# Last attention weights of the second batch: exponentials with a bias by head, then turned, and a new order of work on all engines

## The reference, cut to what matters

```python
q = (x @ Wq).reshape(b, t, h, dh)      # 8 heads of 64
k = (x @ Wk).reshape(b, t, h, dh)
gl_v = (x @ Ws).reshape(b, t, h, e)
wv = _topk_mask(gl_v, 2) * sigmoid(gl_v)
v = einsum('bthe,btek->bhtk', wv, einsum('btd,edk->btek', x, Wv))
scores = einsum('bhid,bhjd->bhij', q * scale, k)
probs = softmax(scores, axis=-1)
attn = einsum('bhij,bhjd->bihd', probs, v)
mask_o = _topk_mask((x @ Wd).reshape(b, t, h, e), 2)
out = einsum('bthe,bthk,ekd->btd', mask_o, attn, Wo)
```

## Time and profile before

| | us |
|---|---|
| median of three runs | 231.01 (230.71 to 776.88) |
| the profiled execution's own time | 230.83 |
| its span in the profile | 229.1 |
| PE busy in the span | 220.0 |
| DVE, ACT, POOL busy | 166.0, 101.1, 93.4 |

### The profile page before, as it was taken

The page is one execution under the profiler, slowest core; times in us unless marked ns, Lnnn a source line. Parts: engine busy times, 40 slices in busy tenths (PEclk is TensorE's granted clock), DMA queues, the critical chain, the costliest instruction groups (busy, mean ns, idle before and its releaser), DMA issues.

```text
span 229.1 us, 3195 instructions
## 1 busy us (share of the span) xinstructions
PE 220.0 (96%) x1192; PEld 167.7 (73%) x1192; DVE 166.0 (72%) x311; ACT 101.1 (44%) x196; POOL 93.4 (41%) x89
## 2 busy tenths in 40 slices
PE   8999999999999899999989999999999699999995
PEld 8998898889888688879474444444557488998963
DVE  2156387767579899981773484899988899698971
ACT  2256425375489497614145245597512202160310
POOL 5104203655566821971025616744863127330000
PEclk9999999999999999999999999999999999999999
DMA  6999859966968973099983298000000000000011
GB/s 235 429 412 399 358 185 451 393 263 215 379 235 318 413 322 137 0 342 419 429 313 150 78 339 363 0 0 0 1 0 3 0 0 3 0 0 4 0 43 49
DMA packets 6639, 43.99 MB, mean 192 GB/s; under 512 B 864, under 2 KB 1376, under 8 KB 1760
## 3 DMA queue, kind: packets, MB, share of 16 engines
q1 hardware_dynamic: 6480, 43.66, 48.2%
q10 hardware_dynamic: 144, 0.13, 0.2%
HBM read 43.27 MB, written 0.52 MB: 191 GB/s over the span
## 4 chain that ended last, share of the span: by engine, by line
PE 69%; DVE 26%; issue 2%; ACT 1%; DVEq 0%; POOL 0%; POOLq 0%
PE psum L412 49%; PE psum L454 16%; DVE ring_r L939 5%; PE psum L428 2%; DVE slots_r L1049 1%; PE psum L416 1%; DVE small L1042 1%; DVE slots L921 1%; DVE slots L1140 1%; ACT slots L1596 1%; PE psum L580 1%; DVE small L911 1%; DVE slots_r L1037 1%; DVE slots L927 1%; DVE psum L1063 1%
## 5 line engine op out<-in xcount | busy, mean ns | idle before, releaser
L412 PE MATMUL psum<-ring_r,slots_r 128*128 128x512 f32 x288 | 69.8, 396 | 2.0 <-DVE slots_r L1109 1.5
L412 PEld LDWEIGHTS psum<-ring_r,slots_r 128*128 128x128 f32 x288 | 53.0, 188 | 15.2 <-ACT slots_r L1596 2.1
L412 PE MATMUL psum<-ring,slots 128*128 128x512 f32 (+5 forms) x170 | 61.4, 513 | 0.7 <-DVE slots L1266 0.5
L1921 POOL TENSOR_TENSOR ring_r<-ring,ring_r 128x640 fp32r<-128x640 f32 x18 | 36.3, 2028 | 43.2 <-ACT ring_r L1596 43.1
L1596 ACT ACTIVATE slots<-psum 128x256 f32<-128x256 f32 (+4 forms) x48 | 20.7, 455 | 71.3 <-PE psum L412 32.4
L412 PEld LDWEIGHTS psum<-ring,slots 128*128 128x128 f32 (+1 forms) x170 | 29.3, 190 | 28.3 <-issue 25.5
L1596 ACT ACTIVATE ring_r<-ring 128x2048 fp32r<-128x2048 f32 x20 | 37.9, 1912 | 7.7 <-PE psum L412 6.8
L454 PE MATMUL psum<-slots,ring 128*128 128x128 f32 x320 | 37.5, 276 | 0.5 <-ACT slots L1596 0.5
L454 PEld LDWEIGHTS psum<-slots,ring 128*128 128x128 f32 x320 | 36.5, 192 | 1.2 <-ACT slots L1596 0.9
L939 DVE TENSOR_TENSOR ring_r<-ring,ring_r 128x1408 fp32r<-128x1408 f32 x18 | 30.2, 1692 | 2.5 <-ACT ring_r L1596 2.3
L1916 POOL TENSOR_TENSOR small<-small,mhalf 128x1 f32<-128x1 f32 x16 | 10.6, 663 | 36.0 <-DVE small L913 34.5
(11 more groups left out here) (184 smaller groups left out, 244.2 us busy)
## 6 DMA issues: line engine op xcount, KB each, us to landing
ring<-blocks SPq DMA_DIRECT2D x36, 1024.0 KB, 8.6
bc<-vecs SPq DMA_DIRECT2D x1, 3072.0 KB, 15.1
bc<-vecs SPq DMA_DIRECT2D x1, 1280.0 KB, 6.6
bc<-vecs SPq DMA_DIRECT2D x1, 512.0 KB, 13.7
slots<-xin SPq DMA_DIRECT2D x1, 256.0 KB, 5.2
y<-slots SPq DMA_DIRECT2D x1, 256.0 KB, 2.0
y<-slots SPq DMA_DIRECT2D x2, 128.0 KB, 1.8
slots<-xin ACTq DMA_DIRECT2D x1, 128.0 KB, 2.7
```

Source lines behind the costliest of these rows:

```text
L412: return t.matmul(o_, l, r, start=first, stop=last)
L1921: g.tensor_tensor(ring_r[:, p, CUT:], ring[:, p, CUT:], ring_r[:, high(name), CUT:], ALU.subtract).then_inc(*split_lowg.inc(name))
```

## The change

Three things are done together.

First, batch 1's last weights are made as batch 0's: `score_t`, `turn_max`, `less_max`, `max_parts`, `select`, `max_turned` and `exp_p` go, with their constants; `max_f`, the exponentials with a bias (`exp_f_`), the turning (`turn_weights`) and the copy out (`weights_out`) serve both batches.

```diff
+            def turn_weights(b, q):
+                s.wait_ge(*exp_f[b].at(str(q)))
                 s.wait_ge(*gates_a[b].at("xv"))
                 s.wait_ge(*gates_a[b].at("k"))
                 s.wait_ge(*gates_v[b].at("gl"))
+                transposes(bank(4 * b + 2 * q), P0[b][:, q * 512:(q + 1) * 512]).then_inc(*sf[b].inc(f"turn{q}"))
...
             def max_f(b, q):
                 s.wait_ge(*sf[b].at(str(q)))
+                v.tensor_reduce(mxf[b][:, 4 * q:4 * q + 4], quarters(4 * b + (1 if q else 3)), AX.X,
+                                ALU.max).then_inc(*own_v.inc())
+                s.wait_ge(*own_v.now())
+                v.tensor_scalar(nmx[b][:, 4 * q:4 * q + 4], mxf[b][:, 4 * q:4 * q + 4], -0.125, None,
+                                ALU.mult).then_inc(*smax_v[b].inc(str(q)))
...
+            def exp_f_(b, q):
+
+                s.wait_ge(*smax_v[b].at(str(q)))
                 for c in range(4):
                     n = 4 * q + c
+                    i = act(P0[b][:, n * 128:(n + 1) * 128],
+                            psum[:, 4 * b + (1 if q else 3), c * 128:(c + 1) * 128], ACT.Exp,
+                            bias=nmx[b][:, n:n + 1], scale=0.125)
+                i.then_inc(*exp_f[b].inc(str(q)))
+
+            def weights_out(b, q):
+                s.wait_ge(*sf[b].at(f"turn{q}"))
+                act(PTf[b][:, q * 512:(q + 1) * 512], bank(4 * b + 2 * q), ACT.Copy).then_inc(*w_out[b].inc(str(q)))
```

Second, the orders of the last block (TensorE, VectorE, ScalarE):

```diff
+            score_f(0, 1)
             score_f(0, 0)
-            score_f(0, 1)
             fk(1)
-            turn_p0(1)
-            turn_p0(0)
+            turn_weights(0, 0)
+            turn_weights(0, 1)
             score_f(1, 0)
+            av(0, 0)
             score_f(1, 1)
             av(0, 1)
-            av(0, 0)
-            turn_max(1)
-            score_t(1)
-            less_max(1)
-            sum_u(0, 1)
+            turn_weights(1, 0)
+            turn_weights(1, 1)
             av(1, 0)
             sum_u(0, 0)
             av(1, 1)
+            sum_u(0, 1)
+            fo(0, 0)
             sum_u(0, 2)
-            fo(0, 0)
             fo(0, 1)
             fo(0, 2)
             sum_u(1, 0)
             sum_u(1, 1)
+            fo(1, 0)
             sum_u(1, 2)
-            fo(1, 0)
...
             p0_turned()
             max_f(1, 0)
+            out_gate(0, 0)
+            gate_out(0, 2, 0)
             max_f(1, 1)
-            max_parts(1)
+            gate_out(0, 0, 0)
             out_gate(0, 1)
-            out_gate(0, 0)
+            gate_out(0, 0, 1)
             gate_out(0, 1, 0)
             gate_out(0, 1, 1)
-            gate_out(0, 0, 0)
-            gate_out(0, 0, 1)
-            gate_out(0, 2, 0)
             gate_out(0, 2, 1)
             out_gate(1, 0)
+            out_gate(1, 1)
+            gate_out(1, 1, 0)
             gate_out(1, 0, 0)
-            gate_out(1, 1, 0)
-            out_gate(1, 1)
             gate_out(1, 0, 1)
             gate_out(1, 1, 1)
+            final(0)
             gate_out(1, 2, 0)
             gate_out(1, 2, 1)
-            final(0)
             final(1)
...
             fq_out(0)
-            exp_p0(0)
-            exp_p0(1)
+            fk_out(0)
             fq_out(1)
+            exp_f_(0, 1)
+            exp_f_(0, 0)
             fk_out(1)
-            select()
-            p0_turned()
-            max_turned(1)
-            exp_p(1, 0)
-            exp_p(1, 1)
+            weights_out(0, 0)
+            exp_f_(1, 0)
+            exp_f_(1, 1)
+            weights_out(1, 0)
+            weights_out(1, 1)
```

Third, the work ahead of the last block is put in another order on all five lists, its amount unchanged: SP's fetches, TensorE's biases, steps and scores, and much of the lists of the others. SP's part from `ct13` on, and TensorE's around `f1(1)`:

```diff
             fetch("ct13")
             fetch("c02")
             fetch("c00")
+            fetch("c01")
             fetch("c11")
+            fetch("c10")
             fetch("c03")
-            fetch("c13")
-            fetch("c10")
             fetch("c12")
             fetch("f1")
+            fetch("f2")
+            fetch("c13")
+            fetch("rg")
+            fetch("ra")
+            fetch("fq")
             fetch("rk")
+            fetch("rv")
+            fetch("ro")
+            s.wait_ge(*used("c12"))
+            fetch("fg")
             s.wait_ge(*used("c11"))
             fetch("rf")
             fetch("rr")
...
             f2(0)
-            s.wait_ge(*normed[1].at("x2"))
-            in_halves(1, "x2", Z[1], 7, 5)
-            f1(1)
-            s.wait_ge(*p_low[1].at("3"))
-            s.wait_ge(*evict[1].at("relu"))
-            bias("a0", 6)
             s.wait_ge(*p_low[0].at("3"))
             s.wait_ge(s_bc1, 16)
             s.wait_ge(*turned[0].at("x2"))
             bias("a0", 1)
+            s.wait_ge(*normed[1].at("x2"))
+            in_halves(1, "x2", Z[1], 7, 5)
+            f1(1)
             turned_rows(0, "n4", N4[0], 0)
             f2(1)
+            step(0, "k", 1, 2)
             step(0, "a", 0, 1, bias_of="a0")
-            step(0, "k", 1, 2)
+            turned_rows(1, "n4", N4[1], 4)
+            s.wait_ge(*p_low[1].at("3"))
+            s.wait_ge(*evict[1].at("relu"))
+            bias("a0", 6)
             s.wait_ge(*normed[1].at("x3"))
             bias("w0", 7)
-            turned_rows(1, "n4", N4[1], 4)
-            step(0, "v", 2, 3, wait=normed[0].at("x3"))
-            step(1, "k", 0, 5, wait=evict[1].at("relu"))
             s.wait_ge(*mixed[0].at("a"))
             s.wait_ge(*mixed[0].at("k"))
             step(0, "r", 3, 0, wait=turned[0].at("n4"))
+            step(1, "k", 0, 5, wait=evict[1].at("relu"))
+            step(0, "v", 2, 3, wait=normed[0].at("x3"))
             step(1, "a", 1, 6, bias_of="a0")
```

More of the change, by code:

```diff
@@ L191, in build @@
         vt2 = [slot(R[b][5]) for b in range(2)]
-        P0 = slot(R[0][0], 2)
+        P0 = [slot(R[b][0], 2) for b in range(2)]
         PTf = [slot(R[b][2], 2) for b in range(2)]
@@ L750, in _ @@
             k1(0)
+            turned_rows(1, "x", Y[1], 4)
             q1(0)
-            turned_rows(1, "x", Y[1], 4)
+            k1(1)
             e1(0)
@@ L789, in _ @@
             scores(1, 3)
-            gather(0, 0)
-            count2(1)
             turn_p(0, 2)
             turn_p(0, 3)
+            count2(1)
+            gather(0, 0)
             shut_out(1)
@@ L1795, in _ @@
             copy_halves(0, "x1", T8, 0, 2)
+            split("ct00")
             out(1, "v1", Vs[1], bank(5))
@@ L1946, in _ @@
                             pattern=[[-1, 128]], channel_multiplier=1).then_inc(*const.inc("ident"))
+            g.memset(mhalf[:, :], -0.5).then_inc(*const.inc("mhalf"))
+            deviation(0, "x")
+            deviation(1, "x")
+            g.memset(causal[:, :], 0.0).then_inc(*own_g.inc())
+            s.wait_ge(*own_g.now())
+            g.affine_select(out=causal[:, :], in_=causal[:, :], compare_op=ALU.is_ge, fill=NEG, base=0,
+                            pattern=[[-1, 128]], channel_multiplier=1).then_inc(*const.inc("causal"))
+            g.memset(pick, 0.0).then_inc(*own_g.inc())
+            g.iota(kidx[:, :], pattern=[[1, 128]], base=0, channel_multiplier=0,
+                   allow_small_or_imprecise_dtypes=True).then_inc(*const.inc("kidx"))
+            low("v1")
+            low("ct01")
+            deviation(0, "x1")
+            low("ct00")
+            g.iota(kidx4[:, :], pattern=[[1, 512]], base=0, channel_multiplier=512,
+                   allow_small_or_imprecise_dtypes=True).then_inc(*const.inc("kidx4"))
+            low("ct02")
             s.wait_ge(*own_g.now())
@@ L1995, in _ @@
             deviation(1, "x2")
-            deviation(0, "x3")
-            deviation(0, "n4")
-            low_third("ro", 0)
             s.wait_ge(*normed[1].at("x2"))
@@ L2001, in _ @@
             mul(x2b[1], Z[1], vec("fc2_b"), x2b_g[1], "x2b", ALU.add)
+            deviation(0, "x3")
+            deviation(0, "n4")
+            low_third("ro", 1)
             deviation(1, "x3")
             deviation(1, "n4")
-            for base in (0, -8):
-                s.wait_ge(*own_g.now())
-                i = g.affine_select(out=sel, in_=sel, compare_op=ALU.not_equal, fill=-1.0, base=base,
-                                    pattern=[[-1, 8]], channel_multiplier=1)
-                i.then_inc(*(const.inc("sel") if base else own_g.inc()))
-            low_third("ro", 1)
+            s.wait_ge(*normed[0].at("n4"))
+            s.wait_ge(s_bc2, 16)
+            mul(X[0], X[0], vec("lnf_b"), x_off[0], "s", ALU.add)
+            g.memset(wbias[:, :], WC).then_inc(*const.inc("wbias"))
             low_third("ro", 2)
+            s.wait_ge(*rk_v[0].at("ys"))
+            mul(sc_[0], ys[0], vec("r_k"), rk_g[0], "sb")
             s.wait_ge(*evict[1].at("k"))
```

429 lines of the change are left out of this document (165 added, 264 removed), and 4 rows, old and new, of the table prod.

## The result

The changed kernel took **234.44 us** (median; 233.78 to 234.93), the kernel before 230.86 in the runs beside it. The ratio is 1.0138 with an interval of 1.0108 to 1.0168: slower by 1.4%, where 230.2 us was forecast, 0.8 less than the 231.01 that the prediction started from. Of the four runs of the kernel before beside it, one of 776.88 stands apart. The profiled execution took 234.68 us.

The account below looks back on a forecast made before the run. TensorE was taken as the bound nearly everywhere. Last block -0.6 and middle -0.2 sum to -0.8: span 229.1 to 228.3, plus 1.73 around it 230.0, plus 0.18 gives 230.2 us (own range 229.4 to 231.2; with rivals 228.4 to 232.6).

Parts of the forecast that it names:

- Last block: Batch 1's new weights path at the end: less TensorE work (-1.73), one wait gone (-0.46), new waits added; -0.6 taken.
- the timetable: Last block's steps on TensorE, VectorE and ScalarE from 204.66, giving waits of 0.35 and 1.05 before batch 1's turns.
- rival 3: VectorE and ScalarE set the end, by scalings of 1.18 or waits per quarter: +1.4 there, 232.2 us; chance 0.17.
- Early: New order in the early part: later `x1` turning against a covered wait before `shut_out(1)`; 0 together, from -0.6 to +0.5.
- The half microsecond for `x1`: Early part: `k1(1)` ahead of `e1(0)` delays `pv1(0)`, so TensorE reaches `x1`'s turning before VectorE has it: +0.5.
- `low_third("rf", 0)` behind `deviation(0, "h")`: GpSimd's order near `h`: the low third still ends before `rf(0)` needs it, by about 0.8 us.
- Middle: One bias fewer ahead of the steps at 131.40: -0.35, of which 0.2 is kept after batch 1's `yg`; bounds -0.5 and +0.5.
- Fetches: Weight blocks behind `fq`, at 423 GB/s: `rr` lands at 129.4, wanted at 131.05; cost 0, 1.7 us of cover.
- the sign named for being wrong about rival 2: TensorE or ScalarE showing a wait for a DMA between 115 and 145 in the changed profile.
- rival 2: Weights behind `fq` land late, below 385 GB/s; at 340 GB/s TensorE waits 2.5, 232.7 us; chance 0.15.
- rival 4: TensorE's clock falls in the waits among transposes; at 1.2 GHz from the turns on, 246 us; chance 0.01.
- The start: Base of the sum: profiled execution's span of 229.1 us, 1.73 around it, and the median 0.18 above it.

Follow-up runs that it names:

- rf_first: Changed kernel with GpSimd's low third of `rf` moved ahead of `deviation(0, "h")` again: 233.17 us, ratio 1.0081.
- weigh_behind: Changed kernel with `weigh2(0)` moved behind `penalty(1)` on VectorE: median of all ten runs 233.31 us, three of them at 235.97 to 236.15.
- pen_h: Changed kernel with `penalty(1)` ahead of `low("c01")` and `weigh2(0)`, and `low_third("rf", 0)` held until VectorE's affine of `h(0)` is done: 231.6 us, ratio 1.0013.
- tail_alone: Kernel before with only the last block changed, everything ahead of it kept: 231.35 us, ratio 0.9982.
- tail_apart: Kernel before with the new last block, GpSimd's `ln3_b` addition earlier and its share of `c00` started after VectorE's: 230.39 us, ratio 0.9955.
- pen_sp: Changed kernel with `penalty(1)` ahead of `low("c01")` and `weigh2(0)`, and the transfers in the order of the kernel before: 236.92 us, ratio 1.0243.
- after_again: The changed kernel measured and profiled once more, nothing altered: 234.5 us, ratio 1.0122.
- early_new: Changed kernel with the old engine order from `f2` to the last block; new transfers and new last block stay: 236.85 us, ratio 1.0231.

## Why the prediction was wrong, step by step

- **Last block: the number right, in part by luck.** -0.6 forecast, -0.58 measured. Two errors cancel. The waits were 0.64, with none before the first four turns and none before `fo(1, 0)`, where 0.35, 1.05 and 0.1 were forecast: 0.86 too much. The work was put too low by 0.97: the row of 16 scores and that of 16 `av` matmuls were halved, but alternating they took 4.26 for the 3.58 of the timetable, and the rest lies in the turns and behind them. The scalings took 0.17, so rival 3 did not occur. Four exponentials took 1.14 for the 1.09 taken from the row of eight. The prediction's 1.17 from the Trainium skill's page "ScalarE: Activation LUTs", section "What ACT_TABLE_LOAD costs", takes off four overlaps; four neighbours have three, which makes the page's estimate 1.27. The clock was full through the transposes (granted clock 1.00 from 209.10 to 210.12 and from 214.38 to 216.20), which does not agree with its page "TensorE: Matmul & The Clock Gate", section "Part 4: PE-mode transpose".
- **Early, "0 together, from -0.6 to +0.5": this is the step that failed.** The half microsecond for `x1` was there (+0.35). But "`count2(1)` and two turns ahead of `gather(0, 0)` cover the wait" looked at TensorE's list alone. The penalty stood behind `weigh2(0)` on VectorE, a move that the prediction does not name and so puts at nothing, and the sum "the amount of work is the same, so only waits count" is false where two engines hold each other: the busy time of VectorE rose from 166.0 to 171.2 and GpSimd's from 93.4 to 97.7 with nearly the same work. Measured +3.6 (1.59 of it the clock) and +3.4 at `x2(0)` in the two profiles of the changed kernel, and +0.6 in rf_first, whose early program is the same and where VectorE was first. The penalty's move alone takes back 1.9 of the median. So with the penalty free the early part costs about the top of the range that I gave; what I left out is the hold between the two engines, 2.8 to 3.0 us here together with the lower clock or the held low part of `c00` beside it.
- **`low_third("rf", 0)` behind `deviation(0, "h")`: failed.** It did end before `rf(0)` needed it, as I wrote. I asked when its result is wanted and not what runs beside it: +0.92 at `h(0)`; held back behind the affine, it gives 1.0 back.
- **Middle: the numbers right, one count not.** -0.35 forecast at the steps, -0.33 measured. But no bias fewer stands ahead of the steps: there are three in either kernel. Counted from `x2(0)`, the first turning of `n4` came 0.59 earlier: one bias less ahead of it, and a wait of 0.48 for one of 0.71. Between it and the steps stand two biases for one, and the wait of 0.24 for a block: 0.26 later. Behind the steps the gain grows to 0.88 by `yg(0)`, as another bias is moved behind, but `yg(1)` is VectorE's, and there it shrinks to 0.10 (forecast 0.2).
- **Fetches: right in the price, not in the cover.** TensorE waited 0.24 for the step of `rr` where 0 with 1.7 of cover was forecast, and ScalarE 1.50 for the block that it splits at 125.96, so the sign named for being wrong about rival 2 did appear. From 115.6, some 2.2 after the last use of `v2`, to the end of that wait the rate was 385 GB/s, not the 423 assumed. Rival 2's price of 2.5 did not appear in the changed kernel, a cost of that size only in the one with the old middle.
- **The clock, rival 4.** It fell in one of the two profiles of the changed kernel, for 1.59 us, and not at the turns but behind the wait before `shut_out(1)`.
- **The start.** The sum started from one execution at the lower of two levels that the kernel before has, 1.1 us apart; I knew of one.

What stays open: why the lower clock came in one execution of the changed kernel and not in others with waits of 1.4 to 1.7 at that place, and where it fell in weigh_behind's three runs of 236 us, of which there is no trace; the 0.7 us by which scores and `av` in turn take longer; and the 0.9 us by which pen_h's early part is still behind that of tail_alone (`x2(0)` at 104.31 for 103.41; both had a held low part of `c00`). At `shut_out(1)` the two are level, 77.98 and 77.95; behind it stands TensorE's wait of 0.62 for a low part, and 0.3 has no cause that I can name.

## What to carry to other kernels

When an order is changed, take for every VectorE instruction that moves not its duration but what GpSimd does during it: beside a GpSimd instruction that adds or subtracts two tensors in SBUF, 0.16 us became 1.55 and 0.49 became 1.8. Look at its form: those that read two tensors from SBUF were held, and the penalty, while small ones with one input and those that read a tensor from PSUM were not. Put nothing that can be held, however small, ahead of the instruction that TensorE waits for, and start the two engines' shares of one block one behind the other rather than with the same event. If a kernel's runs fall into two groups, look for two instructions that start within some tenths of each other.

## What the runs showed of the hardware

- Of a VectorE and a GpSimd instruction that each read two tensors from SBUF, the second is held until the first ends, up to 1.5 us here, and the first keeps its time (VectorE 1.62 with GpSimd 3.03; in weigh_behind VectorE's pair 4.68 with GpSimd 1.57). Where the first is nearly over the hold is short: the low part of 1.62 took 2.29 in tail_alone. The size of the held instruction does not matter: one number per partition was held for 1.4 us, 512 for 1.3. The form does: beside GpSimd's low parts a reduction and a reciprocal of one column kept 0.14 and 0.16 (weigh_behind, 78.00), and a reduction of 128x2048 from PSUM kept 2.29 (changed kernel, 80.64).
- A difference of 0.4 us in when `c00` can be split (66.13 and 66.52) decides which engine is second. Keeping the two apart removed the upper of two levels 1.1 us apart (tail_apart), so I take this for the cause of the levels of the kernel before too, whose upper one was not profiled.
- The granted clock of a stretch fell to 0.67 behind a TensorE wait of 1.78 us and to 0.50, the lower level, behind one of 2.63 (pen_sp); it stayed at 1.00 behind waits of 1.43 and 1.72 before `shut_out(1)` in after_again and early_new.
